# Slot ranks of a mixture of experts by a scan and two matrix products, and similarity products that wait for six row scatters

## The reference, cut to what matters

```python
x = x + _L0_xattn_ref(ctx_512, _layernorm(x), ...)   # two-step graph attention
x = x + _L0_ffn_ref(_layernorm(x), ...)              # top 2 of 8 experts
x = x + _L1_xattn_ref(ctx_512, _layernorm(x), ...)   # learned adjacency from similarities
x = x + _L1_ffn_ref(_layernorm(x), ...)              # attention, top 8 of 32 experts

# _L0_ffn_ref
probs = softmax(x @ w_router);  top_vals, top_idx = top_k(probs, 2)
for e in range(8):
    w_e = sum(where(top_idx == e, top_vals, 0.0), -1)
    h = (silu(x @ w_gate[e] * 0.5) * (x @ w_up[e])) @ w_down[e] * 0.25
    out = out + w_e[:, None] * h

# _L1_xattn_ref
sim = einsum('bhnd,bhmd->bnm', Q, K) / (sqrt(16) * 4)   # Q, K from ctx_512 alone
sparse_mask = sim >= (76th largest of each row)
A_learned = sigmoid(sim) * sparse_mask, made symmetric
```

## Time and profile before

| | |
|---|---|
| median of 3 runs | 1193.59 us (1190.17, 1193.59, 1197.03) |
| profiled execution, its own time | 1190.06 us |
| its span, first to last instruction | 1188.3 us |
| mean granted TensorE clock | 0.925 |
| PE busy | 1068.7 us (90%) |
| DVE busy | 869.6 us (73%) |
| ACT busy | 593.4 us (50%) |
| POOL busy | 433.5 us (36%) |

### The profile page before, as it was taken

One profiled execution on the slowest core, in us unless ns is written; L12 is line 12 of the kernel. 1 busy time (PEld: TensorE's weight loads), 2 busy tenths in 40 slices (PEclk: granted clock), 3 DMA queues, 4 the chain that ended last, 5 costly groups with the idle time before them and its releaser, 6 DMA issues.

```text
span 1188.3 us, 20176 instructions
## 1 busy us (share of the span) xinstructions
PE 1068.7 (90%) x6074; PEld 860.7 (72%) x6074; DVE 869.6 (73%) x2584; ACT 593.4 (50%) x1554; POOL 433.5 (36%) x378
## 2 busy tenths in 40 slices
PE   3988888585999947988999999999998999999997
PEld 2555555363666625877999999999997888888887
DVE  5887777731777556986777777777786988888877
ACT  2656565322333325665778877776784222222221
POOL 2656465126000056862634443222251232333321
PEclk9978786756999978999999999999999999999999
DMA  8900000101112131010101200000000111111111
GB/s 263 353 1 1 1 1 1 60 32 63 45 45 85 49 107 44 2 40 6 36 1 46 62 2 2 1 2 1 1 28 14 41 41 52 48 45 53 40 53 35
DMA packets 55570, 53.58 MB, mean 45 GB/s; under 512 B 5520, under 2 KB 48976, under 8 KB 55488
## 3 DMA queue, kind: packets, MB, share of 16 engines
q1 hardware_dynamic: 52768, 47.27, 12.7%
q0 software_dynamic: 1536, 4.20, 1.1%
q10 hardware_dynamic: 1184, 1.11, 0.3%
HBM read 43.38 MB, written 9.18 MB: 44 GB/s over the span
## 4 chain that ended last, share of the span: by engine, by line
PE 76%; DVE 11%; ACT 4%; issue 3%; POOL 3%; DMA 1%; SPq 0%; DVEq 0%; ACTq 0%; POOLq 0%
PE bank L56 12%; PE bank L57 12%; PE bank L58 12%; PE bank L904 6%; PE bank L925 4%; PE bank L629 4%; PE bank L798 4%; PE bank L806 3%; PE bank L823 3%; PE bank L914 3%; PE bank L612 2%; PE bank L926 2%; DVE g_scale L1580 2%; PE bank L598 1%; POOL x_rows L1341 1%
## 5 line engine op out<-in xcount | busy, mean ns | idle before, releaser
L1376 POOL TENSOR_TENSOR rot_s<-swap,rq 128x512 f32<-128x512 f32 x64 | 89.6, 1401 | 167.4 <-ACT swap L1183 167.2
L1059 ACT ACTIVATE silu<-bank 128x512 f32<-128x512 f32 x66 | 39.4, 597 | 173.7 <-PE bank L58 173.7
L1973 DVE TENSOR_TENSOR o_ring<-bank,o_ring 128x256 fp32r<-128x256 f32 x128 | 54.2, 423 | 88.7 <-ACT o_ring L1214 87.6
L1198 ACT ACTIVATE prob<-prob,pmin 128x128 f32<-128x128 f32 (+1 forms) x256 | 113.2, 446 | 8.2 <-DVE pmin L1954 8.2
L1765 DVE SCALAR_TENSOR_TENSOR xs<-bank,wt,xs 128x256 f32<-128x256 f32 x264 | 109.0, 475 | 0.1
L904 PE MATMUL bank<-kv,norm 128*128 128x128 f32 (+1 forms) x512 | 105.5, 329 | 3.7 <-DVE norm L1947 3.7
L1324 POOL TENSOR_TENSOR gate_r<-gate_w,gate_r 128x256 fp32r<-128x256 f32 x31 | 36.0, 1163 | 175.5 <-ACT gate_r L1052 175.5
L1308 POOL TENSOR_SCALAR rest<-alpha 128x512 f32<-128x512 f32 x32 | 69.0, 2156 | 79.3 <-ACT alpha L997 77.9
L1214 ACT ACTIVATE o_ring<-bank 128x256 fp32r<-128x256 f32 x128 | 48.4, 378 | 83.6 <-PE bank L926 83.5
L1966 DVE TENSOR_SCALAR prob<-prob,pinv 128x128 f32<-128x128 f32 (+1 forms) x256 | 81.3, 362 | 4.5
L56 PE MATMUL bank<-wo_r,o_ring 128*128 128x256 f32 x256 | 84.3, 329 | 0.0
(11 more groups left out here) (291 smaller groups left out, 3178.1 us busy)
## 6 DMA issues: line engine op xcount, KB each, us to landing
gate_w<-in_Wg SPq DMA_DIRECT2D x33, 128.0 KB, 2.1
up_w<-in_Wu SPq DMA_DIRECT2D x33, 128.0 KB, 2.3
down_w<-in_Wd SPq DMA_DIRECT2D x33, 128.0 KB, 2.3
w_all<-in_w_gate SPq DMA_DIRECT2D x8, 512.0 KB, 10.7
w_all<-in_w_up SPq DMA_DIRECT2D x8, 512.0 KB, 10.5
w_all<-in_w_down SPq DMA_DIRECT2D x8, 512.0 KB, 10.7
wq_g<-in_Wq SPq DMA_DIRECT2D x4, 1024.0 KB, 5.0
wo_g<-in_Wo SPq DMA_DIRECT2D x4, 1024.0 KB, 5.8
```

Of the source, the lines that this page charges most:

```text
L1198: ins = act.activation(prob[:, u % 4, nt * P:nt * P + (nt + 1) * P], prob[:, u % 4, nt * P:nt * P + (nt + 1) * P], ACT.Exp, bias=pmin[:, u ...
L1376: pool.tensor_tensor(rot_s[:, m % 2].rearrange("p (b n) -> p b n", b=2), swap[:, m % 2].rearrange("p (b n) -> p b n", b=2), bcast(tab[:, 1 ...
```

## The change

`chosen` becomes a view of a new tile `marks` in which the 8 tiles of an expert lie side by side and a ninth column holds zero. A scan on DVE makes `earlier`: within each expert the running sum of `marks` over the tiles, where `same_e` is 1 and is 0 at each expert's first column, which restarts the sum. PE needs two products: `before` times all 72 columns of `marks`, and `ones` times 64 columns of `earlier`, added one tile further on, so that its last tile gives the counts per expert. The second product waits for the scan (`earlier_done`). The two products read their moving operand with a step of 9 elements. The four clearings (`marks`' last column, `same_e` twice, `padded`) stand ahead of `router0`.

The first six scatters raise `rows_lead` in place of `rows_out`. SyncE waits for both. PE waits for `rows_lead` at 16 x 6 before the first similarity product.

```diff
+LEAD = 6
-        chosen = sb_sparse("chosen", [P, T, E0])
+        marks = sb_sparse("marks", [P, E0, T + 1])
+        earlier = sb_sparse("earlier", [P, E0, T + 1])
+        same_e = sb_sparse("same_e", [P, E0, T + 1])
+        chosen = marks[:].rearrange("p e t -> p t e")[:, 0:T, :]
...
-            sp.wait_ge(S["rows_out"], 16 * K0 * T)
+            sp.wait_ge(S["rows_lead"], 16 * LEAD)
+            sp.wait_ge(S["rows_out"], 16 * (K0 * T - LEAD))
...
             def similarity():
                 pe.wait_ge(S["sim_in"], 48)
+                pe.wait_ge(S["rows_lead"], 16 * LEAD)
...
             def rank_slots():
 
-                marks = chosen[:].rearrange("p t e -> p (t e)")
                 pe.wait_ge(S["before_in"], 16)
                 pe.wait_ge(S["chosen_done"], 1)
-                pe.matmul(bank[3][:, 0:T * E0], before[:, 0:P], marks, start=True, stop=False)
-                for d in range(1, T):
-                    pe.matmul(bank[3][:, d * E0:T * E0], ones[:], marks[:, 0:(T - d) * E0], start=False, stop=d == T - 1)
-                for t in range(T):
-                    mm = pe.matmul(bank[3][:, T * E0:(T + 1) * E0], ones[:], chosen[:, t, :], start=t == 0, stop=t == T - 1)
-                mm.then_inc(S["count_ready"], 1)
+                pe.matmul(bank[3][:, 0:(T + 1) * E0].rearrange("p (t e) -> p t e", e=E0), before[:, 0:P],
+                          marks[:].rearrange("p e t -> p t e"), start=True, stop=False)
+                pe.wait_ge(S["earlier_done"], 1)
+                pe.matmul(bank[3][:, E0:(T + 1) * E0].rearrange("p (t e) -> p t e", e=E0), ones[:],
+                          earlier[:].rearrange("p e t -> p t e")[:, 0:T, :], start=False, stop=True
+                          ).then_inc(S["count_ready"], 1)
...
-                        in_=norm[:, t, :], in_offset=None).then_inc(S["rows_out"], 16)
+                        in_=norm[:, t, :], in_offset=None).then_inc(S["rows_lead" if k * T + t < LEAD else "rows_out"], 16)
...
-                chain.link(dve.memset(padded[:], -1.0))
...
-                dve.tensor_tensor(chosen[:], kept[:, :, 0:E0], padded[:, :, 0:E0], ALU.not_equal).then_inc(S["chosen_done"], 1)
+                dve.tensor_tensor(chosen, kept[:, :, 0:E0], padded[:, :, 0:E0], ALU.not_equal).then_inc(S["chosen_done"], 1)
                 dve.wait_ge(S["chosen_done"], 1)
+                flat2 = lambda a: a[:].rearrange("p e t -> p (e t)")
+                dve.tensor_tensor_scan(flat2(earlier), flat2(same_e), flat2(marks), 0.0, ALU.mult, ALU.add
+                                       ).then_inc(S["earlier_done"], 1)
...
             dve.memset(ones[:], 1.0)
+            chain.link(dve.memset(marks[:, :, T:], 0.0))
+            chain.link(dve.memset(same_e[:], 1.0))
+            chain.link(dve.memset(same_e[:, :, 0:1], 0.0))
+            chain.link(dve.memset(padded[:], -1.0))
             router0()
```

More of the change, by code:

```diff
@@ L288, in build @@
             "zero_done", "wa_done", "sd_done", "row_zeroed",
-            "chosen_done", "count_ready", "slot_done", "owner_done", "rows_out",
+            "chosen_done", "earlier_done", "count_ready", "slot_done", "owner_done", "rows_lead", "rows_out",
             "xg_turned", "xgT_copied", "gate_ready", "up_ready", "gact_done", "hid_done",
@@ L1648, in router0 @@
                 chain.link(dve.engine_nop())
-                dve.tensor_tensor(chosen[:], kept[:, :, 0:E0], padded[:, :, 0:E0], ALU.not_equal).then_inc(S["chosen_done"], 1)
+                dve.tensor_tensor(chosen, kept[:, :, 0:E0], padded[:, :, 0:E0], ALU.not_equal).then_inc(S["chosen_done"], 1)
                 dve.wait_ge(S["chosen_done"], 1)
+                flat2 = lambda a: a[:].rearrange("p e t -> p (e t)")
+                dve.tensor_tensor_scan(flat2(earlier), flat2(same_e), flat2(marks), 0.0, ALU.mult, ALU.add
+                                       ).then_inc(S["earlier_done"], 1)
                 weight, place, rank = (spread[:, j] for j in range(3))
                 count, tiles, end, start = (tally[:, j, :] for j in range(4))
-                dve.scalar_tensor_tensor(weight, chosen[:], 0.25, padded[:, :, 0:E0], ALU.mult, ALU.mult)
+                dve.scalar_tensor_tensor(weight, chosen, 0.25, padded[:, :, 0:E0], ALU.mult, ALU.mult)
                 dve.wait_ge(S["count_ready"], 1)
@@ L1662, in router0 @@
                     ALU.mult, ALU.add))
-                chain.link(dve.scalar_tensor_tensor(rank, place, 1.0, chosen[:], ALU.add, ALU.mult))
+                chain.link(dve.scalar_tensor_tensor(rank, place, 1.0, chosen, ALU.add, ALU.mult))
                 dve.tensor_reduce(last[:, 0, :], rank, X, ALU.max)
```

## The result

| | before | changed |
|---|---|---|
| median of 19 runs each, us | 1193.51 (1189.31 to 1197.03) | 1186.92 (1182.16 to 1190.75) |
| profiled execution, its span | 1190.06, 1188.3 | 1189.45, 1187.7 |
| mean granted clock | 0.925 | 0.927 |

The ratio is 0.9945, 95% interval 0.9934 to 0.9957: 6.6 us faster, with 5.1 to 7.9 in the interval. The forecast was 1186.5, 5.4 us under a base of 1191.9.

The account below looks back on a forecast made before the run. No engine is busy throughout; the chain that ended last, three quarters PE, bounds the kernel. Ranks and clearing -6.10 us plus late similarities 0.7 give -5.4, so 1191.9 - 5.4 = 1186.5 us; 8-in-10 range 1181 to 1193.

Parts of the forecast that it names:

- The ranks: Chain from `chosen` to the slots: fewer PE rank records save 5.90 us, clearing `padded` off the chain 0.20, together 6.10.
- the rival of the dear step: Rank products reading with a step of 9 cost 3.0 us more: -2.4 us, 1189.5 us; chance 0.09.
- The scan: New DVE operation before PE's second rank product: hidden behind the first product's records; uncovered it would cost 0.23 us.
- The hold: PE's wait for six scatters before the similarity products: their last copy delays the mixture's first turn by 0.7 us.
- The rival of the free hold: Similarities need 14.7 us or less, so PE's wait for six scatters costs nothing: -6.1 us, 1185.8 us; chance 0.14.
- GpSimd's scaling: Scaling of `sig` behind the scatters and low weights: would start at 279.3 without waiting, 1.0 us to spare.
- The sum: Shift of the mixture's first turn, let through whole to the end: -6.10 + 0.7 = -5.4 us.
- The clock: PE's clock through the held similarity products: stays at 0.50, so the mixture's first tile runs at 1.2 GHz as now.
- The rule that I weighed: Sustained PE activity releases the clock, giving the mixture full clock at its start: -8.4 us, 1183.5 us; chance 0.10.
- The rival of the late clock: Clock rises later in the mixture, each further tile at 0.50 costing 5.8 us; with three 1203.9 us; chance 0.06.
- The base: Whole-kernel time before the change, taken as the middle of four executions: 1191.9 us.

Follow-up runs that it names:

- the run with the ranks only: The changed kernel without PE's wait for the first six scatters before the similarity products: 1186.68 us, ratio to before 0.9950.
- the hold of twelve: The changed kernel with the similarity products held until twelve scatters have landed in place of six: 1194.4 us, ratio to before 1.0000.
- the added products: Changed kernel without PE's wait for scatters, unread products before the mixture: ten, 1187.54 us; eleven plus one of 256 columns after the first turn, 1182.94 us.

## Why the prediction was right

**The ranks.** Predicted 6.10 us to the counts, measured 11.33 - 5.24 = 6.09. The product with 72 columns at a step of 9 took 0.67 us for two records, beside 0.66 before, and the second one added 0.43 for a forecast of 0.42. That settles the rival of the dear step: it asked for 3.0 us. The parts on DVE were a little off both ways. With the step `chosen` took 0.27 us in place of 0.23, and `rank`, which reads it, 0.27 in place of 0.22, so the first scatter gained 6.05:

```profile
257.81 0.22 DVE L1663 SCALAR_TENSOR_TENSOR spread<-spread,chosen 128x64 f32<-128x64 f32 x1
```

```profile
253.95 0.27 DVE L1670 SCALAR_TENSOR_TENSOR spread<-spread,marks 128x64 f32<-128x64 f32 x1
```

The first row is before, the second the changed kernel. The scan took 0.31, within the bounds, and ended at 251.75, 0.28 us ahead of PE's second product, so it was hidden. That product started 0.48 after the first where the records of before stood 0.45 apart; the 0.03 lies between the first product's own two records, and whether the step or the 8 more columns cost it is not shown. The Trainium skill ("DVE: opcode table, instruction layouts, handler registers and perf-mode slots", section "6. Datapath and trigger behaviour") says that this scan runs at half throughput; 0.308 us for 72 elements beside 0.226 for an operation of 64 agrees in direction, though the longer operation explains a part.

**The hold.** Predicted late by 0.7, measured 33.12 - 32.31 = 0.81. The copy of the last similarity ended 15.36 us after the first projection, 15.38 before. Both ends came later than forecast. The hold's came 0.33 later, by waits that I had put too short: 0.17 from the landing to PE, which I had at nothing, and 0.25 from ACT's copy to PE, which I had at 0.1. The load's came 0.22 later, so the extra is 0.1 only. The rival of the free hold fell with it, since ACT ended the wait in both traces. GpSimd's scaling did not wait, as computed: it followed the low weights at once, at 281.63.

**The sum.** Forecast for the first turn -5.4, measured 33.12 - 38.19 = -5.1; 0.1 of the rest is the hold and 0.2 what the load's end lost, by the operations on DVE and a load of 2.10 instead of 1.99 as the run with the ranks only shows it. Over two traces each the third turn, behind the clock's rise, moved from 50.28 to 44.87, -5.4; that this is the forecast's figure is luck, for in the two traces of the changed kernel the clock rose 2.96 and 5.49 us after the gate began, where it was 4.80 and 4.81 before. The interval of the time, 5.1 to 7.9, has the -5.4 in it and the -5.1 at its edge; where the rest of the 6.6 arises no trace shows, since from the third turn to the end the changed kernel's two took as long as those of before or longer. That a shift here reaches the end whole, which I had only assumed, is borne out by the hold of twelve within some 3 us either way.

**The clock.** The step that the added products and the traces bear out is that the held products leave the clock at 0.50: 15 us of busy PE in the changed kernel, as in the earlier trace rows before. The rule that I weighed, that of the Trainium skill ("TensorE: Matmul & The Clock Gate", section "What's actually happening") by which activity releases the clock, does not forecast this: the held products, with 64 rows in the array, left it at 0.50, and the added ones of 128x128 by 512 columns were followed by 1.00 within 4 us. The measurement decides; why the two differ stays open. The rival of the late clock did not happen: the rise came 2.96 to 5.69 us after the first gate began in all kernels without added products.

**The base.** The profiled 1190.06 lay 3.5 us under the median; the middle of four executions, 1191.9, was still 1.6 under the later median of 1193.51. That the forecast of the time was off by 0.4 us only is two small errors that cancel, 1.6 of the base and 1.2 of the difference.

## What to carry to other kernels

Products as small as these, some 0.21 us a record at half clock from 8 columns to 72, are priced by the piece: count records, not elements. A wait that is added to hold work back must be followed to its end, through every engine behind it, and set beside what it was to be hidden under; here the two ends lay 0.8 us apart, and only the row that names who ended the wait told which came last. Idle time of PE ahead of a dense stage can be filled with products of 128x128 by 512 columns, which bought 2 us at the third turn here, but only where the stage behind it waits for PE.

## What the runs showed of the hardware that I had not expected

A good part of the spread between executions arises ahead of the change: the router's first reduction, which waits for products that no kernel here changes, came between 239.46 and 249.21 us in ten traces, with the low clock there in other places in nearly all of them. Up to it the clock was at 0.50 for 87.5 us in the earliest and for 119.7 in the latest, but for 92.4 only in the next to latest, so the low clock alone doesn't give the order. From the third turn to the end the traces lie between 892.8 and 897.4.

The clock fell for 3.4 us at the opening of the last mixture, where PE waits 1.8 us in every trace, in all three traces that have both the new ranks and the hold, and in none of the seven others; the stretch to the end was 1.6 us longer there (294.4 to 294.5 against 292.8 to 292.9 us from the first silu of that mixture on). Whether that is the hold's doing or chance stays open. If it is the hold's, its price is 2.4 us and not 0.8, and the medians of 1186.68 and 1186.92 with and without it don't show that.
